# Seven products over the whole depth in three of five steps, with the block transposes moved behind the third gate

## The reference, cut to what matters

```python
Af = A.astype(prop_state.dtype); AfT = Af.T          # 2048 x 2048, 0/1, symmetric in these inputs
for _ in range(N_STEPS):                             # 5
    s_in = state @ in_W.T + in_b;  s_out = state @ out_W.T + out_b
    a = concatenate([Af @ s_in, AfT @ s_out, state], axis=-1)
    r = sigmoid(a @ r_W.T + r_b);  z = sigmoid(a @ z_W.T + z_b)
    joined = concatenate([Af @ s_in, AfT @ s_out, r * state], axis=-1)
    h_hat = tanh(joined @ h_W.T + h_b)
    state = (1.0 - z) * state + z * h_hat            # 2048 x 256
out = tanh(state @ o1_W.T + o1_b) @ o2_W.T + o2_b
x = layernorm(x + out)
```

## Time and profile before

| | us |
|---|---|
| median of three runs | 661.55 (661.32 to 661.77) |
| the profiled execution, device time | 660.54 |
| its span, first to last instruction | 658.7 |
| TensorE busy | 647.0 (98%) |
| VectorE busy | 481.5 (73%) |
| ScalarE busy | 407.1 (62%) |
| GpSimd busy | 51.1 (8%) |
| transfers on SyncE's queue, share of 16 engines | 25.9% |

### The profile page before, as it was taken

How to read it: one execution, slowest core, us unless ns; L and a number is a source line. 1 busy time by engine, 2 the same in 40 slices (tenths; PEclk the granted TensorE clock), 3 DMA queues, 4 the chain that set the end, 5 groups by cost and what they waited for, 6 DMA issues and landing times.

```text
span 658.7 us, 8626 instructions
## 1 busy us (share of the span) xinstructions
PE 647.0 (98%) x2908; PEld 535.6 (81%) x2908; DVE 481.5 (73%) x782; ACT 407.1 (62%) x544; POOL 51.1 (8%) x49
## 2 busy tenths in 40 slices
PE   8999999999999999999999999999999999999994
PEld 7888888787888888888888888888888888888884
DVE  4986988897487569838784994677489658725887
ACT  2765554479457747855593788368368935763646
POOL 0191126100400000000000000000000000000002
PEclk9999999999999999999999999999999999999998
DMA  8998757222000221300013031000312200013003
GB/s 289 354 354 218 183 193 170 35 52 46 0 1 33 57 40 36 52 8 0 32 39 57 0 68 28 0 32 32 54 43 64 33 1 0 2 65 127 1 0 132
DMA packets 106803, 48.30 MB, mean 73 GB/s; under 512 B 88976, under 2 KB 95248, under 8 KB 106512
## 3 DMA queue, kind: packets, MB, share of 16 engines
q1 hardware_dynamic: 98256, 46.82, 25.9%
q10 hardware_dynamic: 8512, 1.05, 1.1%
HBM read 33.69 MB, written 11.53 MB: 69 GB/s over the span
## 4 chain that ended last, share of the span: by engine, by line
PE 95%; DVE 3%; issue 1%; ACT 0%; POOL 0%; DVEq 0%; POOLq 0%
PE bank L593 26%; PE bank L580 17%; PE bank L582 17%; PE bank L581 17%; PE bank L646 16%; PE bank L742 2%; PE bank L771 1%; DVE stats L1629 1%; DVE a L1622 0%; DVE deg_sum L1251 0%; DVE ring L1184 0%; PE bank L818 0%; ACT a L1168 0%; DVE work L1662 0%; DVE stateT L1228 0%
## 5 line engine op out<-in xcount | busy, mean ns | idle before, releaser
L593 PE MATMUL bank<-ring,rows 128*128 128x512 f32 x768 | 178.6, 389 | 0.0
L941 ACT ACTIVATE work<-work,bias 128x512 f32<-128x512 f32 x120 | 85.9, 722 | 149.1 <-DVE work L1349 148.5
L593 PEld LDWEIGHTS bank<-ring,rows 128*128 128x128 f32 x768 | 144.1, 188 | 30.1 <-issue 0.2
L1349 DVE SCALAR_TENSOR_TENSOR work<-degree,deg_w,bank 128x512 f32<-128x512 uint16 x120 | 88.6, 745 | 54.7 <-PE bank L582 53.9
L841 ACT ACTIVATE ring<-a 128x1024 fp32r<-128x1024 uint8 (+1 forms) x115 | 116.3, 1048 | 8.8 <-PE bank L593 6.6
L580 PE MATMUL bank<-u_c,fold 128*128 128x512 f32 x240 | 93.5, 390 | 0.0
L582 PE MATMUL bank<-u_c,fold 128*128 128x512 f32 x240 | 93.4, 389 | 0.0
L581 PE MATMUL bank<-u_c,fold 128*128 128x512 f32 x240 | 93.4, 389 | 0.0
L646 PE MATMUL bank<-ring,rows 128*128 128x512 f32 x256 | 65.1, 391 | 0.0
L580 PE MATMUL bank<-st_c,own 128*128 128x512 f32 x160 | 62.4, 390 | 0.3 <-DVE st_c L1184 0.3
L581 PE MATMUL bank<-st_c,own 128*128 128x512 f32 x160 | 62.3, 389 | 0.0
(11 more groups left out here) (150 smaller groups left out, 921.5 us busy)
## 6 DMA issues: line engine op xcount, KB each, us to landing
stage<-in_adj_dram SPq DMA_DIRECT2D x15, 512.0 KB, 8.3
sums<-in_adj_dram SPq DMA_DIRECT2D x13, 512.0 KB, 5.9
turned_dram<-work SPq DMA_DIRECT2D x12, 512.0 KB, 2.6
rows<-turned_dram SPq DMA_DIRECT2D x192, 32.0 KB, 2.0
work<-in_x_dram SPq DMA_DIRECT2D x4, 512.0 KB, 10.6
x_dram<-work SPq DMA_DIRECT2D x4, 512.0 KB, 10.1
a<-x_dram SPq DMA_DIRECT2D x4, 512.0 KB, 5.3
a<-in_adj_dram SPq DMA_DIRECT2D x3, 512.0 KB, 11.0
```

Of the source, the lines that this page charges most:

```text
L593: m = nc.tensor.matmul(u_bank[2 * (c % 2) + d][:, :], rows[:, part, j, d * P:(d + 1) * P], tile[:, jj, :], start=(first and jj == 0 and pa ...
L941: nc.scalar.activation(gates[:, g, e, :], gates[:, g, e, :], ACT.Tanh if g == H else ACT.Sigmoid, bias=bias[:, g, e:e + 1]).then_inc(gate_ ...
L1349: nc.vector.scalar_tensor_tensor(out=gates[:, g, e, :], in0=degree[:, c * CW:(c + 1) * CW], scalar=deg_w[:, g, e:e + 1], in1=g_bank[s % 3] ...
```

## The change

Steps 2 to 4 do the second half of the depth with seven products too; step 1 keeps the old scheme under new names (`HALF_ORDER`, `half_aggregate`, `half_mix`). A side of steps 2 to 4 has 28 tiles of four matmuls. ScalarE still expands 20 of them, VectorE 8 instead of 2: the four P5 tiles, and the last two tiles of P2 (`tensor_copy`) and of P7 (`tensor_scalar`). The weights of the second half are differences of the row blocks of chunks 2 and 3 (L1 to L4, `l_add`); they lie in `rows`, `u_c` and `rs_c`, are kept in DRAM for side 1 (`keep_late`, `load_late`), and their raw forms are made in the R and Z gate buffers (`spare`, `keep_l11`). The byte sums for four pairs (side, half of the depth) are made in step 1 by GpSimd, kept in DRAM (`store_sums`) and loaded ahead of each side (`load_sums`, two transfers of 768 KB). `own_part` of gates 0 to 2 of chunks 0 and 2 is moved ahead into the aggregate (`own_ahead`; in step 1 to its end). `split_state` of chunks 2 and 0 is moved into the gate stages of chunks 1 and 3, behind gate 3. `turn_state` of an updated chunk is moved behind gate 2, which is the third one. The row blocks of chunk 1 are split in side 0, not before it. T4 and T3 are formed behind gate 4 of chunk 2. P4 and P5 get places of their own (`t_bank`, a copy `copy_p5`). Packing instructions are moved out of the gates of chunk 0 in steps 1 to 3. In the loops of PE and ScalarE step 1 is written out, and the loop covers steps 2 and 3.

```diff
+    ORDER = [(P1, 0), (P1, 1), (P6, 0), (P6, 1), (P7, 0), (P7, 1), (P4, 0), (P4, 1), (P1, 2), (P1, 3), (P5, 0), (P5, 1),
+             (P5, 2), (P5, 3), (P2, 0), (P2, 1), (P3, 0), (P3, 1), (P6, 2), (P6, 3), (P2, 2), (P2, 3), (P3, 2), (P3, 3),
+             (P7, 2), (P7, 3), (P4, 2), (P4, 3)]
+    OWN_AT = {ORDER.index((P1, 2)): (0, 1), ORDER.index((P6, 2)): (2,)}
+    OWN_AHEAD = 3
+    BY_VECTOR = [n for n, (kind, p) in enumerate(ORDER) if kind == P5 or kind in (P2, P7) and p >= 2]
+    ROWS = [(T1, 0), (T2, 0), ("b11", 0), (T3, 0), (T4, 0), (L11, 0), (L1, 0), (1, 0), (1, 1),
+            (L2, 0), (L21, 0), (L22, 0), (L3, 0), (L4, 0)]
 # PE, aggregate_pair
+                    if n in OWN_AT:
+                        own_ahead(t, 2 * side, OWN_AT[n])
+                    if side == 0 and p % 2 == 0:
+                        pe.wait_ge(row_lo, row_count(t, NEEDS[kind, p]))
+                    if side == 1 and (kind, p) == (P6, 2):
+                        pe.wait_ge(late_back, 32 * (t - 1))
 # PE, gate_chunk
-                    wait(pe, gate_read, t * S_GATE + c * GATE + s - 2)
-                    own_part(g_bank[s % 3], g, e, st_c)
+                    if first or c % 2 or s >= OWN_AHEAD:
+                        wait(pe, gate_read, t * S_GATE + c * GATE + s - 2)
+                        own_part(g_bank[s % 3], g, e, st_c)
 # ScalarE, aggregate_pair of steps 2 to 4
+                for k in range(4, 8):
+                    cast(t, side, k)
+                if side == 0:
+                    keep_l11(t)
+                    row_high(t, L11, 0)
+                cast(t, side, 8)
+                if side == 0:
+                    turn_move(t - 1, range(2))
+                cast(t, side, 9)
+                if side == 0:
+                    turn_move(t - 1, range(2, 4))
+                    row_high(t, L1, 0)
+                    for h in range(2):
+                        row_high(t, 1, h)
+                copy_p1(t, side)
...
 # ScalarE, gate_chunk_two
                 gate(t, c, 3)
+                if not ending:
+                    for e in range(DB):
+                        split_state(*((t, 2) if c == 1 else (t + 1, 0)), e)
 # VectorE, gate_chunk
-                    if not last:
-                        turn_state(t, c - 1)
                     rs_low(t, c, 0)
                     rs(t, c, 1)
...
                 gate(t, c, 2)
+                if (c == NC - 1 or c == 1 and not first) and not last:
+                    turn_state(t, c - 1)
                 rs_low(t, c, 1)
...
+                if c == NC - 1 and not last or c == 1 and not first:
+                    for e in range(DB):
+                        split_state(*((t, 2) if c == 1 else (t + 1, 0)), e)
 # VectorE, aggregate_pair of steps 2 to 4, side 0 (side 1 has test() in its places)
+                update(*old)
+                    turn_state(*old)
+                    l_add(t, L1)
+                    row_low(t, L11, 0)
+                cast(t, side, 0)
+                cast(t, side, 1)
+                    row_low(t, L1, 0)
+                    for h in range(2):
+                        row_low(t, 1, h)
+                cast(t, side, 2)
+                cast(t, side, 3)
+                for _ in range(4 if side else 2):
+                    test()
+                    l_add(t, L2)
+                    l_add(t, L4)
+                    row_low(t, L2, 0)
+                    row_low(t, L21, 0)
+                    l_add(t, L3)
+                cast(t, side, 4)
+                cast(t, side, 5)
+                    for k in (L22, L3, L4):
+                        row_low(t, k, 0)
+                mix(t, side, V)
+                cast(t, side, 6)
+                cast(t, side, 7)
+                mix(t, side, C12)
+                for d in range(DB):
+                    split_u(t, 2 * side, d)
+                mix(t, side, U3)
```

More of the change, by code:

```diff
@@ new lines, in groups, with order, by_act, by_vector @@
+    def groups(t, side, per_half, per_full, ahead=0):
+        if half(t):
+            return side * per_half + ahead
+        return t * (2 * per_full) + (ahead + side * per_full + 2 * per_half - 4 * per_full)
+    def order(t):
+        return HALF_ORDER if half(t) else ORDER
+    def by_act(t):
+        return HALF_BY_ACT if half(t) else BY_ACT
+    def by_vector(t):
+        return HALF_BY_VECTOR if half(t) else BY_VECTOR
+    def mixed_at(t, side, what):
+        return groups(t, side, len(HALF_MIXES), len(MIXES), (HALF_MIXES if half(t) else MIXES).index(what) + 1)
@@ L89, in row_count, with sums_loads, used_at, rows_ahead_of @@
+    def sums_loads(t, side):
+        return t * 32 + 16 * (side - 1)
+    def used(t, side):
+        return groups(t, side, HALF_NI, NI, S_PAIR)
+    def used_at(t, side, kind, p):
+        return used(t, side) + (order(t).index((kind, p)) + 1)
+    def rows_ahead_of(t):
+        return HALF_ROWS[2:7] if half(t) else ROWS[2:5]
     def row_count(t, op):
-        return t * NROW + (ROWS.index(op) + 1 - NROW)
+        if half(t):
+            return HALF_ROWS.index(op) + 1
+        return t * NROW + (ROWS.index(op) + 1 + len(HALF_ROWS) - 2 * NROW)
@@ L463, in _ @@
             turn_move(0)
+            for side in range(2):
+                store_sums(side, 0)
             for t in range(1, LAST):
+                if t > 1:
+                    keep_late(t)
+                    load_sums(t, 1)
                 turn_store(t, 0)
+                if t > 1:
+                    load_late(t)
                 turn_store(t, 1)
-                for k in range(2):
-                    turn_load(t, k)
+                turn_load(t, 0)
+                if t == 1:
+                    store_sums(0, 1)
+                turn_load(t, 1)
+                if t == 1:
+                    store_sums(1, 1)
+                load_sums(t + 1, 0)
                 if t == LAST - 1:
@@ L478, in _ @@
                 turn_move(t)
-            sp.wait_ge(pair_used, used(LAST, 1) + ORDER.index((P3, 1)) + 1)
+            keep_late(LAST)
+            load_sums(LAST, 1)
+            load_late(LAST)
+            sp.wait_ge(pair_used, used_at(LAST, 1, P3, 1))
             sp.dma_start(t_flat[:, 0:4 * DB * D].bitcast(F32), o_dram).then_inc(o_back, 16)
@@ L642, in aggregate_pair @@
                         if (kind, p) == (P3, 0):
-                            pe.wait_ge(mixed, groups(t, side, 6, W5))
+                            pe.wait_ge(mixed, mixed_at(t, side, W5))
                         for jj in range(2):
                             for part in (HI, LO):
-                                last = nc.tensor.matmul(u_bank[BANK[kind]][:, :], product_rows(kind, part, 2 * p + jj), tile[:, jj, :],
+                                last = nc.tensor.matmul(u_bank[HALF_BANK[kind]][:, :], half_rows(kind, part, 2 * p + jj), tile[:, jj, :],
@@ L660, in aggregate_pair, with product_rows @@
                     last.then_inc(pair_used, 1)
+                own_ahead(t, 2 * side, range(OWN_AHEAD))
+            def product_rows(product, part, p, jj):
+                j = 2 * (p % 2) + jj
+                cols = slice(j * P, (j + 1) * P)
+                b = 2 * BC * (p // 2)
+                if product in (P1, P5):
+                    d = (P1, P5).index(product)
+                    return rows[:, part, b + j, d * P:(d + 1) * P]
+                if product in (P2, P3):
+                    d = (P2, P3).index(product)
+                    return rows[:, part, b + BC + j, d * P:(d + 1) * P]
+                if p < 2:
+                    return t_rows[:, part, (P6, P7, P4).index(product), cols]
+                return {P6: u_c[:, part, 0, cols], P7: rs_c[:, part, 1, cols], P4: rs_c[:, part, 0, cols]}[product]
@@ L820, in _ @@
             step(0, first=True)
-            with pe.Fori(1, LAST) as t:
+            step(1)
+            with pe.Fori(2, LAST) as t:
                 step(t)
@@ L1143, in _ @@
             step(0, first=True)
-            with act.Fori(1, LAST) as t:
+            step(1)
+            with act.Fori(2, LAST) as t:
                 step(t)
@@ L1186, in cast @@
             def cast(t, side, k):
[L1188 to L1189 removed]
+                n = by_vector(t)[k]
+                kind, p = order(t)[n]
                 dve.wait_ge(pair_used, used(t, side) + n - RING + 1)
[L1191 to L1194 removed]
+                h = p // 2
@@ L1400, in next_pair @@
                         store_pair(c + 2, p)
-                    elif not first and (c == 0 or c == 1 and last):
+                    elif last and c < 2:
                         test_symmetry(t, 2 * DB * c + p)
@@ L1417, in next_rows @@
                         return
-                    for what, k in ROWS_AT[c, n]:
+                    for what, k in ROWS_AT[c, n] or [("low", op) for op in rows_ahead_of(t + 1)]:
                         if what == "add":
@@ L1528, in aggregate_pair @@
                     row_low(t, 2, 1)
-                test()
-                test()
-                for e in range(DB):
```

(5 more changed lines are left out.)

383 lines of the change are left out of this document (304 added, 79 removed).

## The result

| | before | after |
|---|---|---|
| median, us | 661.72 (661.32 to 662.87) | 665.25 (664.58 to 666.29) |
| ratio to before, 95% interval | | 1.0051 (1.0038 to 1.0064) |
| the profiled execution, us | 660.54 | 666.29 |
| its span | 658.7 | 664.5 |
| mean granted clock | 0.995 | 0.993 |

Both columns are of six executions. The changed kernel is 3.5 us slower, by more than the 0.2% that a measurement can tell. The forecast was 659.7 us and its range ended at 664.5: the sign was wrong, and the range did not hold the time.

The account below looks back on a forecast made before the run. TensorE's matmul count bounds steps 1 to 4. 660.54 us (profiled) - 10.9 for 48 matmuls + 7.2 for the late row block + 1.8 for step 1 = 658.7; the median lies 1.0 above: 659.7 us, range 652.0 to 664.5.

Parts of the forecast that it names:

- rival (5): Whole kernel: the change does not do what it says, matmuls stay at 2908; no chance given.
- (1): Side 0: rows come by 6.3 us, no tile waits; 650.7 us, with step 1's loss 652.5; chance 0.14.
- (2): Side 0: shorter hand-overs, rows at 7.5 us, wait of 1.2 us per side; 656.1 us; chance 0.16.
- rival (3): Side 0: one-source casts take 1.21 us, so tiles 24 and 25 are late too; 662.1 us; chance 0.13.
- late row block: Side 0, steps 2 to 4: chunk 2's rows come late, tile 13 waits 2.4 us, 7.2 us in three sides.
- the cover of side 1's casts: Side 1: no row blocks, casts come in order 0.4 us or more ahead of TensorE; put at nothing.
- Part (b): Chunk 3: rs_low, rs and gate 2 go ahead of the transposes, and VectorE stands 0.8 us; 2.7 us later.
- Step 1's two waits: Start of step 1: TensorE should wait at tiles 4 and 5 for ScalarE.
- (a): Chunk 2, 54 matmuls long with VectorE's work unchanged: gate 5 begins 2.8 us into chunk 3, 1.6 us later than before.
- Edits at nothing: Side 1's casts, moved packing, SyncE's queue and transfers, GpSimd's added sums and u_c's last part: no cost.
- step 1's loss: Start of step 1: two split_state and the wait of (b) make tiles late; 1.8 us, bounds 0 to 2.8.
- Rival (4): Chunks 2 and 3: larger VectorE backlog, 0.1 us more per hand-over; 664.1 us; decides from transposes 4.8 us later; chance 0.15.

Follow-up runs that it names:

- e9: Changed kernel with five edits: transposes ahead of rs_low, step 1's split back, GpSimd's third sums later, casts of tiles 12 and 13 first, gate 2's own_part back; 650.07 us.
- e5: Changed kernel with GpSimd's third set of sums begun only after VectorE's two P5 casts in side 1 of step 1; 663.87 us.
- e8: Changed kernel with own_part of gate 2 left in chunk 2's gates in side 1, six matmuls moved back; 660.76 us.
- e6: Changed kernel with VectorE's casts of tiles 12 and 13 ahead of chunk 1's two row_low; 662.28 us.
- e3: Changed kernel with the transposes one gate later still, behind gate 3; 670.23 us.
- e4: Changed kernel with chunk 0's two split_state for step 1 taken back into step 1's side 0; 663.43 us.
- e2: Kernel before with only the transposes moved behind gate 2; 662.52 us, ratio 1.0012.

## Why the prediction was wrong

**What held.** 48 matmuls, 10.9 us: e9 has it all. The count of 2860 excludes rival (5), the waits rivals (1) and (2). The one-source casts took 0.69 us for the 0.63 of the forecast, so rival (3) is out; the rule of the Trainium skill that the prediction weighed there ("VectorE: DVE Perf Modes", What auto-detection actually checks) is borne out by these rows. The mechanism of the late row block held, with its tiles and its three sides 0, and so did the cover of side 1's casts in steps 2 to 4. Side 1 waits all the same, which the prediction named as a sign of being wrong (58.69 us for its 58.0): not for casts or sums, but 0.7 to 0.8 us in chunk 3, where the prediction had 0.3. Part (b) is right to the tenth: from gate 5 to the transposes VectorE takes 9.2 us, before 6.5, 2.7 later. Step 1's two waits stand at tiles 4 and 5.

**The late row block: 2.4 us a step predicted, 3.4 measured (10.1 for 7.2 in all).** The mechanism was right and its size was not. Take the start of side 0 as it would be without the waits of chunk 3, 271.34. The prediction had the rows there 8.7 us behind it; it was 9.6. Of the 0.9 missing, 0.3 are in (a): gate 5 comes 3.1 us into chunk 3 and came 1.2 in before, 1.9 later for 1.6. The other 0.6 are in the way from the transposes to the rows, 12.3 us for 11.7. The store and the issuing of the loads took what the earlier trace rows show; but VectorE saw the rows 1.9 us after the last load was issued, where I had 1.35, from the end of a busy DMA slice and 0.2 on top. The profile has the landing itself. For the last load of that stretch of the kernel before (issue from 389.00), and for the one of the changed kernel (issue from 278.54):

```profile
DMA to landing us min/median/max: 1.8/1.8/1.8
DMA to landing us min/median/max: 2.4/2.4/2.4
```

So 390.8 was read rightly. But over the twelve row blocks of the kernel before the last load lands 1.8 to 2.4 us after its issue began, and the forecast took one value, the shortest, without bounds. From the rows to tile 13 it took 8.3 us for 8.2. That is 17.9 for the 14.5 at which TensorE wants the tile, and the smaller waits before it do lie inside. The other two steps are alike (3.5 and 3.3).

**Edits at nothing: 0 predicted, 2.2 measured.** Two of them were not nothing. GpSimd's added sums were put at nothing because they "hold only SyncE's stores"; I looked at who waits for GpSimd, not at whom GpSimd disturbs. They cost 1.3 us (e5). The trace of before could not price this: GpSimd's sums of the earlier trace rows never lay beside a cast that PE wanted. The Trainium skill states the rule that I passed over, "SBUF — State Buffer", Who interferes with whom: VectorE's instructions with both inputs in SBUF contend with those of GpSimd that read SBUF. The rows of step 1 agree on every point: casts with two SBUF inputs 4.29 us for two instead of 2.35, the one with a PSUM input at 0.68 as ever, GpSimd's at 2.16 instead of 1.29. That page of the Trainium skill ("Terms") goes further, to a lock that is held for the full instruction; the ends in turn, 1.08 to 1.16 us apart, fit that, and GpSimd's row of 216.93, which began first, has its usual 1.04 us. The other was chunk 2 of step 4, 0.9 us, in side 1: the backlog was counted only for what it does to the transposes, and step 4 has none; but the gates of the shortened chunk wait for VectorE all the same (e8).

**The clock: 0 predicted, 1.7 us in the profiled execution.** The prediction took step 1's loss as 1.8 and left the clock alone. The waits were right: 3.56 less 1.7 is 1.9, and e6, which has the waits and no half clock, has 2.1. Whether the fall follows is another matter. e5 and e8 start step 1 at the same 146.84 and wait alike (tile 4 starts at 151.96 and 151.97, tile 5 at 153.48 in both); in e5 the clock fell behind them, in e8 it did not. Of the five kernels whose profile has both waits, 1.5 us or more and 0.5 (after, e3, e5, e6, e8), it fell in two, and in none of the others. So it was seen only behind these waits, and what decides stays open. For the median it counts for less than in the profiled execution, 665.25 against 666.29: the mean granted clock was 0.993 in the profiled one and 0.994 to 0.996 in the five others. Of e4's 1.8 us the waits are 1.2 (the 2.4 of e6 and e8 less 1.22); the 0.6 left (0.4 against the kernel before) can be the clock of some executions or chance.

**Why the sign turned.** The forecast had 9.0 us of losses against 10.9 of gain, a margin of 1.9. The measured losses are 15.8 in the profiled execution: 2.9 more than forecast for the row block, 2.2 for what was put at nothing, 1.7 for the clock. Either of the first two alone uses up the margin, so the sign would have turned without the clock too. Rival (4) was the nearest: its point of decision was transposes 4.8 us later than before, they were 4.6 later (13.6 for 9.0), and it gave 664.1. But it laid everything on the hand-overs between VectorE and ScalarE, which were nearly right, and had no room for GpSimd, step 4 or the clock. That is the fault of the range: nearly every cost that I did not know could only add to a sum which already had no slack in side 0, and its upper end stood only 4.8 us above the forecast.

## What to carry to other kernels

Where a change takes work from the bound engine and gives it to its helpers, write down for each moved piece its slack in the new stage, not the old one: moving the transposes cost 1.1 us in the kernel before (e2) and 8.3 in the changed one, where their rows were wanted a few tiles earlier and the chunk ahead of them was shorter. For every instruction added on an engine that "nobody waits for", ask whom it runs beside: starting GpSimd's sums 3.8 us later, behind the two casts that TensorE needs (e5), gave back 1.4 us. When the losses nearly eat a gain, look for the order that removes them before giving up the change: five small reorderings turned +0.5% into -1.8%.

## What the runs showed of the hardware

- Two-input casts of VectorE beside GpSimd: 4.29 us for two instead of 2.35, its packing instructions 6.27 us for four instead of 2.7 (0.69 each before); GpSimd's two-tensor sums 2.16 us instead of 1.29. The two engines' instructions end in turn, 1.08 to 1.16 us apart. An input from PSUM: no change.
- A one-source cast of 1024 bytes to fp32r on VectorE: 0.69 us, as long as a two-input operation on 512; a two-input one on 1024 takes 1.22.
- A store of 512 KB and 16 loads of 32 KB each behind it, from the last producer to the first reader: 12.3 us, of which the store is 2.6, the issuing of the loads 7.7 and the landing behind the last issue 1.9. From the start of its issue the last load landed after 1.8 to 2.4 us in the twelve row blocks of the kernel before.
- TensorE's granted clock went to half for 3.41 us after waits of 1.5 and 0.5 us in the profiled executions of two kernels, and stayed at full after waits as long or longer in three others.
- The start of step 1 lay between 145.9 and 147.1 us, and the end behind step 4 between 32.5 and 33.5 us, over twelve kernels whose code there is nearly the same: differences of one us in a single profiled span are not to be explained.
